# Two of GpSimd's normalised image blocks move ahead of the next image's hats, and image 1's first group product moves some slots down

## The reference

```python
def _gn(v, G=32, eps=1e-05):                 # group norm, 4 channels a group
    ...
x = x + _L0_conv_ref(_gn(x), ...)            # per channel: the normed image times a gate
x = x + _L1_conv_ref(_gn(x), ...)            # attention over a neighbourhood

def _L0_conv_ref(x, w_offset, w_deform, b_deform):
    pooled = jnp.mean(x, axis=(2, 3))
    offset = conv(pooled, w_offset)          # three taps over channels
    p = clip(index + tap + offset)           # deformed positions
    samp = g0 * (1.0 - frac) + g1 * frac     # linear interpolation of pooled
    gate = sigmoid(sum_k samp * w_deform + b_deform)
    return x * gate

def _L1_conv_ref(x, ...):
    value = conv1x1(x)                       # 64 channels
    keyf, query = proj(x), proj(x)           # two 1x1 convolutions with norm and relu each
    # keys and values at 3x3 offsets of dilations 1, 2 and 4: 27 taps
    sim = softmax(sum_c(unfold(keyf) * query), over the taps)
    context = sum(sim * unfold(value), over the taps)
    return conv1x1(context)
```

## Time and profile before

| | |
|---|---|
| median of 3 runs | 1492.63 us (1491.96 to 1493.38) |
| the profiled execution | 1492.62 us, span 1490.9 us |
| busy, share of the span | PE 97%, PEld 79%, DVE 84%, ACT 78%, POOL 62% |
| chain that ended last, by engine | PE 71%, POOL 18%, issue 5%, ACT 3%, DMA 1% |
| chain, GpSimd's lines | L863 6%, L797 5%, L796 2%, L800 1%, L799 1%, L811 1% |
| DMA | 138 GB/s on average, the 16 DMA engines 46% busy |

### The profile page before, as it was taken

One profiled execution on the slowest core, in us unless ns is written; L12 is line 12 of the kernel. 1 busy time (PEld: TensorE's weight loads), 2 busy tenths in 40 slices (PEclk: granted clock), 3 DMA queues, 4 the chain that ended last, 5 costly groups with the idle time before them and its releaser, 6 DMA issues.

```text
span 1490.9 us, 34971 instructions
## 1 busy us (share of the span) xinstructions
PE 1449.1 (97%) x9123; PEld 1183.3 (79%) x9123; DVE 1248.9 (84%) x4602; ACT 1169.6 (78%) x3047; POOL 918.9 (62%) x2049
## 2 busy tenths in 40 slices
PE   5899999999999999999999999999999999999998
PEld 2688888888888888888888888888888888888886
DVE  7688888888888888888888888888888888888776
ACT  3687878788778788878887878878887888787886
POOL 5675567575566675566665576665576765575730
PEclk9999999999999999999999999999999999999999
DMA  3235554345554345554345554445544455544344
GB/s 139 71 103 154 158 162 124 112 143 162 155 162 123 110 145 167 151 157 117 119 147 169 154 146 110 133 151 169 153 130 112 144 153 164 158 123 116 98 116 144
DMA packets 104706, 205.95 MB, mean 138 GB/s; under 512 B 13632, under 2 KB 83776, under 8 KB 96448
## 3 DMA queue, kind: packets, MB, share of 16 engines
q1 hardware_dynamic: 103632, 203.49, 45.9%
q10 hardware_dynamic: 880, 0.23, 0.1%
HBM read 51.62 MB, written 51.38 MB: 69 GB/s over the span
## 4 chain that ended last, share of the span: by engine, by line
PE 71%; POOL 18%; issue 5%; ACT 3%; DMA 1%; DVE 0%; SPq 0%; POOLq 0%; ACTq 0%; DVEq 0%
PE ps_s L447 18%; PE ps_o L480 14%; PE ps_v L519 10%; PE ps_t L459 8%; PE ps_p L496 8%; PE ps_p L501 8%; POOL xb L863 6%; POOL hats L797 5%; PE ps_o L485 2%; POOL hats L796 2%; ACT hats L689 2%; POOL hat_sum L800 1%; POOL hat_sum L799 1%; POOL of_x L811 1%; PE ps_v L542 1%
## 5 line engine op out<-in xcount | busy, mean ns | idle before, releaser
L618 ACT ACTIVATE e<-e,zmin 128x256 f32<-128x256 f32 x800 | 402.9, 504 | 161.1 <-DVE zmin L1002 157.4
L1002 DVE CUSTOM_DVE_ANT_0 e<-ps_s,mask 128x256 f32<-128x256 f32 x800 | 337.1, 421 | 162.8 <-PE ps_s L447 155.1
L480 PEld LDWEIGHTS ps_o<-eT,v 128*128 128x128 f32 x2688 | 380.6, 191 | 83.3 <-issue 70.6
L480 PE MATMUL ps_o<-eT,v 128*128 128x128 f32 x2688 | 430.5, 275 | 0.4 <-ACT eT L633 0.3
L447 PE MATMUL ps_s<-kk,qq 128*128 128x256 f32 x1408 | 427.8, 386 | 0.0
L863 POOL TENSOR_SCALAR xb<-raw,g 128x32 f32<-128x32 f32 (+3 forms) x768 | 372.0, 499 | 0.0
L459 PE MATMUL ps_t<-ident,e 128*128 128x128 f32 x1600 | 305.7, 273 | 0.0
L459 PEld LDWEIGHTS ps_t<-ident,e 128*128 128x128 f32 x1600 | 225.3, 141 | 80.6 <-issue 0.2
L633 ACT ACTIVATE eT<-ps_t 128x512 f32<-128x512 f32 (+1 forms) x416 | 236.7, 569 | 64.8 <-PE ps_t L459 61.5
L1019 DVE SCALAR_TENSOR_TENSOR e<-e,rz,keep 128x256 f32<-128x256 f32 x480 | 250.2, 521 | 17.1
L447 PEld LDWEIGHTS ps_s<-kk,qq 128*128 128x128 f32 x1408 | 223.5, 192 | 47.0 <-issue 40.9
(11 more groups left out here) (143 smaller groups left out, 1629.1 us busy)
## 6 DMA issues: line engine op xcount, KB each, us to landing
out_dram<-raw SPq DMA_DIRECT2D x32, 1568.0 KB, 5.6
raw<-in_x_dram SPq DMA_DIRECT2D x31, 1568.0 KB, 6.7
v<-v SPq DMA_DIRECT2D x192, 224.0 KB, 2.9
kk<-kk SPq DMA_DIRECT2D x192, 112.0 KB, 2.1
ksp<-kk SPq DMA_DIRECT2D x192, 64.0 KB, 2.1
v<-v_last SPq DMA_DIRECT2D x64, 128.0 KB, 2.9
kk<-kk SPq DMA_DIRECT2D x32, 224.0 KB, 2.9
v<-v_last SPq DMA_DIRECT2D x64, 96.0 KB, 2.7
```

What stands on the lines that cost most here:

```text
L480: last = nc.tensor.matmul(o[:, UPIX * (u - 1):UPIX * (u + 1)], v[:, s, u, :], eT[:, UPIX * (base + 2 * u - 1):UPIX * (base + 2 * u + 1)], ...
L618: nc.scalar.activation(e[:, i, :], e[:, i, :], ACT.Exp, bias=zmin[:, i:i + 1], scale=-1.0, accum_out=zs[:, i:i + 1]).then_inc(e_done.next( ...
L1002: nc.vector.tensor_tensor_reduce(e[:, i, :], ps_s[(TILES * n.parity() + t) % 2][:, 0:KEYS], mask[:].rearrange("p s h a b -> p (s h a b)"), ...
```

## The change

GpSimd's blocks get a slot table of their own. Against the slots before, only blocks 4 and 5 move: from -2 and -1 to -6 and -5, slots 19 and 20 of the image before, ahead of step p4 in slot 21. Image 1's own chain table gets other entries: c1 from 13 to 16, d1 from 14 to 16, p3 from 15 to 17, c3 from 19 to 20 (d4 stays at 20).

```diff
 V_SLOT = [-8, -7, -4, -1, 4, 7, 10]
+BLOCK_SLOT = [-14, -13, -10, -9, -6, -5, 4]
...
-CH_OF = {0: dict(CH, d6=22), 1: dict(CH, d6=29, a6=29, d7=30, p7=30, c4=31, d9=31, p11=33, pw=34)}
+CH_OF = {0: dict(CH, d6=22), 1: dict(CH, c1=16, d1=16, p3=17, c3=20, d4=20, d6=29, a6=29, d7=30, p7=30, c4=31, d9=31, p11=33, pw=34)}
...
                         for m, rel in items_at(n, t):
                             for b in range(COLUMNS):
-                                if rel == V_SLOT[b // 2 * 2] - 6 + b % 2:
+                                if rel == BLOCK_SLOT[b]:
                                     spread(m, b)
```

## The result

The changed kernel took 1481.52 us (median of 4 runs, 1480.2 to 1482.46) against 1492.3 us: 10.8 us less, ratio 0.9926 with the interval 0.9914 to 0.9937. The direction was right; the time lies above the range of 1467 to 1477, and the gain is half of the 22.1 us forecast. The profiled execution took 1480.2 us, span 1478.5. In the changed kernel every line from 53 on is one higher than before: L542 is L543 now, L519 is L520, L1102 is L1103.

What follows compares the result with a forecast made beforehand. TensorE, busy 97% of the span, bounds the kernel, and GpSimd's order counts only where TensorE waits for it. Steady -18.5 and ramp -3.6 sum to -22.1 us, from 1492.6 to 1470.5 us, range 1467 to 1477.

Steps and rivals of the forecast that it cites:

- The wait of L542, 0.61 us: TensorE's weight load waits for GpSimd's L814; 0.61 us an image goes, by a margin of 0.22 us, 18.5 us in all.
- Blocks 4 and 5 at cost 0: The six block instructions, 3.12 us, fit in GpSimd's idle time before the hats and cost 0.
- The work behind L542 comes 0.61 us earlier, too: TensorE's work after L542, such as the next tile's scores, was taken to meet no new wait: 0.
- it follows: VectorE, busy 36.64 of 43.68 us, was claimed to keep up with TensorE's earlier work: 0.
- Rival (b): Another wait on TensorE takes all of the 0.61 us, only the ramp's 3.6 stay: 1489.0 us, chance 0.03.
- Rival (c): Blocks 4 and 5 collide with VectorE's step d4, and hats and p7 slip: 1498.9 us, chance 0.02.
- move earlier and cost nothing: GpSimd's x1 strips and block 6 behind step p7 run earlier, at a cost of 0.
- The ramp, -3.6 us: Start of the kernel, once: -3.67 - 1.71 + 1.1 + 0.7 = -3.6 us.
- The 3.67 us wait: In image 0, TensorE's product from blocks 4 and 5 waits 3.67 us for them; all of it goes.
- The entries of image 1: Image 1's later chain steps delay the values of blocks 0 and 2 in the ramp: 1.1 us, bounds 0.3 and 2.0.
- the clock: The slow stretch from 54.86 to 60.98 us runs at full clock: 1.71 us less, 0 if the clock falls anyway.
- rival (a): VectorE's d7 holds p7 back, 0.26 of 0.61 us stay each image: 1478.3 us, chance 0.13.

Runs made afterwards that it cites:

- e3: The changed kernel with block 4's value product in slot 5 in place of 4: 1470.75 us, ratio 0.9851 to the kernel before.
- e6: The changed kernel with VectorE's copy of the group product's result (d9) ahead of the scaling L1020, from image 2 on: 1480.17 us, ratio 0.9925.
- e2: The kernel before with only image 1's chain table changed, blocks 4 and 5 left behind the hats: 1494.99 us against 1492.85, ratio 1.0014.
- e13: The changed kernel itself, nothing altered, run again beside another kernel on the same chip: 1481.77 us, ratio 0.9931.

## Why the prediction was wrong

**The wait of L542, 0.61 us: right.** From 44.96 to 44.35 us is what e3 shows once nothing else stands in the way, and 18.5 us from image 1 to image 31 is the forecast's term. The margin was there, too: L815 ended at 811.09, over 0.6 us before L543's start at 811.76. It was larger than the 0.22 us of the sum, since the L1020 ahead of d7 no longer meets the blocks, as the prediction said.

**Blocks 4 and 5 at cost 0: right.** They took 2.72 us in GpSimd's idle time, and the hats came no later.

**The step that failed** is "The work behind L542 comes 0.61 us earlier, too. The scores of the next tile need VectorE's pass over the tile two before [...] I take 0 for both". It looked at one of the products behind L542 and at one of VectorE's results. The value product of slot 4 needs another, the copy of L542's own result, and the code said so (`held`, the wait on dg for d9). Most of its size could be read from the trace of before:

```profile
820.93 0.17 DVE L1102 COPY in_x<-ps_v 128x6 f32<-128x6 f32 x1
...
821.50 1.06 PE L519 MATMUL ps_v<-wvoT,xb 128*128 128x128 f32 x8
```

The copy follows VectorE's L1019 (820.44 to 820.94) without a gap and ends at 821.10, so it can't come earlier. Without its wait L542 would start near 820.0 and the value product 0.88 us behind it (the distance from 807.40 to 808.28 in e3's rows), at 820.9. A product starts 0.25 us after the end of the copy that it waits for (812.67 to 812.92), so at 821.35: by this estimate a wait of some 0.4 us. The price of the step was set to 0; it measured 0.37 us an image, 11 us in all. That is nearly the whole shortfall of 11.3 us: 10.2 of the steady 18.5 us did not come. And "it follows" fails a second time behind it: with the copy's wait gone and VectorE's work left in place, L502 waits for what hangs on VectorE's row minimum, 0.29 us an image in e6.

**Rival (b)**, that the wait moves on, was the true case with 0.37 of the 0.61 us; the prediction had it only for the whole, with a chance of 0.03. The argument against it was a stretch between two waits with TensorE full. But that stretch was full behind a wait of 0.61 us, which put the value product (821.50) 0.4 us behind the copy's end: a full engine downstream of a wait is no evidence for what happens without the wait. A part of the 0.61 us staying should have been in the sum or among the rivals.

**Rival (c)**, the collision of blocks with step d4: it did not occur. The blocks ended at 797.66, and d4's first instruction, L1073, starts at 797.99; one scaling in slot 19 (L1017) took 0.57 us for 0.35, where VectorE has the room. The collision that did occur is elsewhere. GpSimd, released earlier, now runs its strips of slots 2 and 3 beside VectorE's L1020 of slot 3. The prediction said that they "move earlier and cost nothing"; they cost 0.27 of the 0.37 us. The Trainium skill, page "SBUF — State Buffer", section "Who interferes with whom", names the two partners rightly, an instruction of VectorE with two SBUF inputs and one of GpSimd that reads SBUF. It also says that the later one is blocked for the whole instruction. The two strips from 811.61 take 0.79 us each, so that L1020, started at 811.85, would have lost the 0.55 us to the end of the first strip; it lost 0.75 - 0.48 = 0.27. The measurement decides: half of the rule's price in this pair, as far as the listed times of GpSimd, which are rough, can tell. That the collision itself costs time is plain: between 100 and 1400 us of the changed kernel's trace, each of the 87 L1020 that met no GpSimd instruction took 0.48 or 0.49 us.

**The ramp, -3.6 us: right in kind, and in sum partly by luck.** The 3.67 us wait is gone:

```profile
51.01 1.06 PE L520 MATMUL ps_v<-wvoT,xb 128*128 128x128 f32 x8
...
55.76 1.02 PE L502 MATMUL ps_p<-hid,w2T 128*128 128x448 f32 x2 [0.96 <-ACT hid L642]
57.18 0.36 PE L543 MATMUL ps_v<-of_x,group_avg 128*128 128x6 f32 x2 [0.40 <-POOL of_x L815]
57.43 0.67 PE L448 MATMUL ps_s<-kk,qq 128*128 128x256 f32 x2
```

The value product of slot 4 runs at 51.01. New is a wait of 0.96 us for ScalarE that was not forecast, and L543's wait is 0.40 us in place of 0.7. The entries of image 1 cost 1 to 3 us for 1.1. As for the clock, the two traces with a wait of 3.6 us or more ahead of this value product (the kernel before and e2) have 0.66 and 0.50 from 56 to 61 us, and the ten with the blocks moved have 1.00 there. But seven of these ten have 0.50 to 0.75 from 36 to 41 us, and the profiled execution is not one of them. Another execution of the same kernel, e13, gave 61.12 - 59.97 = 1.15 us in the ramp and not 3.7, and the medians, 10.8 us apart, leave about 2.

**The range** had a slip in its lower end: with the terms that it names, -18.5 - 3.67 - 1.71 + 0.3 gives 1469.0 and not 1467. The upper end, 1474 by its terms and 1477 with rival (a), held nothing for the failed step.

## What to carry to other kernels

When a wait on the bound engine is taken away, go through every instruction behind it, not the next one only: what does each wait for, and when is that done if it does not move with the bound engine? Where the helper works without a gap, its results don't move, and each reader that comes earlier meets them. An idle time that two waits share is paid out only when both are gone, so an edit that gives nothing alone (the value product one slot later, on the kernel of before) can be worth 11 us after another. There may be a third behind the second: here the copy's wait, removed by itself, gave back 0.08 of 0.37 us. And a helper that is released earlier runs its other work earlier, too, beside instructions that it did not meet before.

## What was not expected of the hardware

TensorE's clock in the ramp is not set by the kernel alone. Two executions of the changed kernel have granted clocks of 1.00 and of 0.96 and 0.50 (a little of the time and all of it at 1.2 of 2.4 GHz) over the same 10 us. First the profiled execution of the result, then that of e13:

```profile
31.00:36.00 5.00, 2.50 (x5) 0.89 (x6) 3.28 (x7) 2.15 (x4) 5.00 (x12) 1.00 0.04 10
36.00:41.00 5.00, 3.77 (x21) 2.59 (x20) 1.58 (x5) 2.15 (x4) 4.36 (x13) 1.00 0.07 17
```

```profile
31.00:36.00 5.00, 2.51 (x5) 1.05 (x6) 3.27 (x7) 2.15 (x4) 5.00 (x12) 0.96 0.04 10
36.00:41.00 5.00, 4.48 (x14) 2.90 (x13) 1.35 (x4) 0.64 (x1) 4.35 (x13) 0.50 0.06 13
```

Columns: us, busy PE, PEld, DVE, ACT, POOL, granted clock, DMA share, GB/s. TensorE idled as much in both ahead of the fall. The scores behind image 1's group product start at 57.43 us in the one and at 59.97 us in the other, 2.5 us for nothing that the kernel does. The clock also goes with the spread of the runs: those of the changed kernel with 0.998 or 0.999 over the span took 1479.9 to 1480.6 us, those with 0.995 or 0.997 took 1481.8 to 1483.3. What decides it between two executions stays open.
